# Three groups of lag between cumulative sums and their count, rests ahead of floors, and router parts on Pool

## The reference

```python
rates = relu(x) * 0.001
c = cond[:, None, :] + cumsum(rates, axis=1)
fl = floor(c)
spikes = (fl - concat([floor(cond)[:, None], fl[:, :-1]], axis=1)) / 0.001
logits = spikes.reshape(2048, 256) @ router_w.T
# softmax, the two best experts of each row, a capacity for each expert,
# gelu(rows @ w1[e]) @ w2[e], weighted by the gates and added up
out = x + ffn(spikes)
```

## Time and profile before

| | us |
|---|---|
| median of the runs | 63.9 (63.8 to 64.32) |
| the profiled execution | 64.14 |
| its span, first to last instruction | 62.4 |
| TensorE busy | 52.4 (84%) |
| VectorE busy | 34.9 (56%) |
| ScalarE busy | 27.5 (44%) |
| Pool busy | 18.9 (30%) |
| mean granted TensorE clock | 0.91 |

### The profile page before, as it was taken

The page is one execution under the profiler, slowest core; times in us unless marked ns, Lnnn a source line. Parts: engine busy times, 40 slices in busy tenths (PEclk is TensorE's granted clock), DMA queues, the critical chain, the costliest instruction groups (busy, mean ns, idle before and its releaser), DMA issues.

```text
span 62.4 us, 1154 instructions
## 1 busy us (share of the span) xinstructions
PE 52.4 (84%) x372; PEld 30.5 (49%) x372; DVE 34.9 (56%) x157; ACT 27.5 (44%) x46; POOL 18.9 (30%) x59
## 2 busy tenths in 40 slices
PE   3999999999665679999999999999999999993000
PEld 1315255546122343334296679966796666570000
DVE  3399469994677966799889529590320034036000
ACT  0499459775256779146025003940199930000000
POOL 6799875200002170064867500000000000001830
PEclk9999999999999555555699999999999999999996
DMA  0399999999999995002679834999999999200130
GB/s 0 83 365 336 345 326 366 336 360 336 349 348 347 348 348 183 16 5 66 171 250 260 289 132 92 294 362 301 364 350 354 388 384 394 95 0 0 50 98 11
DMA packets 13545, 14.82 MB, mean 238 GB/s; under 512 B 648, under 2 KB 13040, under 8 KB 13536
## 3 DMA queue, kind: packets, MB, share of 16 engines
q1 hardware_dynamic: 12608, 12.62, 62.0%
q0 software_dynamic: 816, 2.01, 10.5%
q10 hardware_dynamic: 112, 0.07, 0.5%
HBM read 13.08 MB, written 2.36 MB: 248 GB/s over the span
## 4 chain that ended last, share of the span: by engine, by line
PE 59%; DMA 11%; DVE 10%; issue 6%; ACT 4%; POOL 3%; ACTq 1%; POOLq 0%; DVEq 0%
PE bank L710 23%; PE bank L694 12%; DMA w_got<-in_L_ffn_w_dram,w_index 7%; DMA router_rows<-in_L_ffn_router_w_dram 5%; PE bank L534 4%; POOL out_dram L522 3%; PE bank L565 3%; PE bank L555 2%; PE bank L574 2%; DVE floors L963 2%; PE bank L726 2%; PE bank L545 2%; PE bank L562 2%; ACTq L797 1%; PE bank L727 1%
## 5 line engine op out<-in xcount | busy, mean ns | idle before, releaser
L534 PE MATMUL bank<-ones_b 128*128 128x512 bf16 x33 | 14.5, 568 | 1.1 <-POOL ones_b L422 1.1
L710 PE MATMUL bank<-w_sb,spare_sb 128*64 128x256 f32 x128 | 14.7, 382 | 0.0
L710 PEld LDWEIGHTS bank<-w_sb,spare_sb 128*64 128x64 f32 x128 | 8.8, 137 | 4.5
L522 POOL DMA_INDIRECT out_dram<-floors,out_index x2 | 2.0, 1016 | 22.6 <-DVE floors L1164 22.3
L853 ACT ACTIVATE spare_sb<-bank 128x512 f32<-128x512 f32 x8 | 4.6, 592 | 8.5 <-PE bank L694 8.5
L694 PE MATMUL bank<-ev_pair,w_got 128*128 128x128 f32 x64 | 7.8, 278 | 0.1
L694 PEld LDWEIGHTS bank<-ev_pair,w_got 128*128 128x128 f32 x64 | 7.4, 192 | 0.7 <-DMA w_got<-in_L_ffn_w_dram,w_index 0.7
L1071 DVE TENSOR_SCALAR rate<-bank,pair_gate 128x256 f32<-128x256 f32 x4 | 1.9, 484 | 9.5 <-PE bank L710 9.5
L503 POOL DMA_INDIRECT w_got<-in_L_ffn_w_dram,w_index x4 | 4.1, 1023 | 5.5 <-DVE w_index L1060 4.9
L534 PEld LDWEIGHTS bank<-ones_b 128*128 128x128 bf16 x33 | 3.2, 119 | 4.4 <-issue 3.2
L812 ACT ACTIVATE x_hi<-x_sb 128x512 fp32r<-128x512 f32 x7 | 4.2, 623 | 1.5 <-DMA x_sb<-in_x_dram 1.5
(11 more groups left out here) (220 smaller groups left out, 80.2 us busy)
## 6 DMA issues: line engine op xcount, KB each, us to landing
w_sb<-in_L_ffn_w_dram SPq DMA_DIRECT2D x8, 1024.0 KB, 10.9
x_sb<-in_x_dram SPq DMA_DIRECT2D x8, 256.0 KB, 5.9
out_dram<-x_sb SPq DMA_DIRECT2D x1, 2048.0 KB, 14.0
cond<-in_cond_dram ACTq DMA_DIRECT2D x2, 32.0 KB, 2.2
w_got<-in_L_ffn_w_dram,w_index POOLq DMA_INDIRECT x4, 5.2
cond<-in_cond_dram SPq DMA_DIRECT2D x1, 32.0 KB, 1.9
x_rows<-in_x_dram,out_index POOLq DMA_INDIRECT x2, 3.7
out_dram<-floors,out_index POOLq DMA_INDIRECT x2, 2.8
```

What stands on the lines that cost most here:

```text
L534: nc.tensor.matmul(bank[2][:, 0:4 * P], ones_b[:, :], ones_b[:, :].unsqueeze(1).to_broadcast([P, 4, P]), start=True, stop=True)
L710: mm = nc.tensor.matmul(Y[d % 2][at, :], hT[:, d % 2, f, at], w2_sb[:, 2 * d + side, f, :], start=(f == 0), stop=(f == FC - 1))
```

## The change

TensorE's order, ScalarE's order and VectorE's order in the sum stage are written anew, and the five router operations move from VectorE to Pool, behind the indirect DMA of line 487 and ahead of `more_lists`. `weigh(g)` now follows `cumulate(g + 3)`. The number of matmuls, rests and floors is the same. On Pool each of the five operations waits for the one before by a semaphore of its own, and the first by `router_out`, which VectorE's copy of the router sets; that copy now stands ahead of `take_rests(1)`.

```diff
+    LAG = 3
...
+            pool.wait_ge(router_out, 1)
+            g.tensor_scalar(router_s[:, :, :], routerT[:, :, :], SPIKE, 0.0, ALU.mult, ALU.add).then_inc(router_parts, 1)
+            pool.wait_ge(router_parts, 1)
+            g.tensor_copy(router3[:, 0, :, :], router_s[:, :, :]).then_inc(router_parts, 1)
+            pool.wait_ge(router_parts, 2)
+            g.tensor_tensor(router_r[:, :, :], router_s[:, :, :], router3[:, 0, :, :], ALU.subtract).then_inc(router_parts, 1)
+            pool.wait_ge(router_parts, 3)
+            g.tensor_copy(router3[:, 1, :, :], router_r[:, :, :]).then_inc(router_parts, 1)
+            pool.wait_ge(router_parts, 4)
+            g.tensor_tensor(router3[:, 2, :, :], router_r[:, :, :], router3[:, 1, :, :], ALU.subtract).then_inc(router3_set, 1)
             pool.wait_ge(counts_set, 1)
...
             for g in range(XG):
                 cumulate(g)
-                if g:
-                    weigh(g - 1)
-            weigh(XG - 1)
+                if g >= LAG:
+                    weigh(g - LAG)
+            for g in range(XG - LAG, XG):
+                weigh(g)
...
             take_rates(3)
+            take_rates(4)
             sign_floors(1)
-            take_rates(4)
             take_rates(5)
...
-            take_rests(1)
-            take_floors(0)
-            take_rests(2)
             dve.wait_ge(router_t, 1)
             v.tensor_copy(routerT[:, :, :], bank[5][:, 0:KC * E].rearrange("p (k e) -> p k e", k=KC)).then_inc(router_out, 1)
+            take_rests(1)
+            take_rests(2)
             take_rests(3)
+            take_floors(0)
+            take_rests(4)
+            take_rests(5)
             take_floors(2)
-            take_rests(4)
-            dve.wait_ge(router_out, 1)
-            loose(v.tensor_scalar(router_s[:, :, :], routerT[:, :, :], SPIKE, None, ALU.mult))
-            take_rests(5)
-            dve.wait_ge(vec, steps[0])
-            loose(v.tensor_copy(router3[:, 0, :, :], router_s[:, :, :]))
+            take_rests(6)
+            take_rests(7)
             take_floors(4)
-            dve.wait_ge(vec, steps[0])
-            loose(v.tensor_tensor(router_r[:, :, :], router_s[:, :, :], router3[:, 0, :, :], ALU.subtract))
-            take_rests(6)
-            dve.wait_ge(vec, steps[0])
-            loose(v.tensor_copy(router3[:, 1, :, :], router_r[:, :, :]))
-            take_rests(7)
-            dve.wait_ge(vec, steps[0])
-            v.tensor_tensor(router3[:, 2, :, :], router_r[:, :, :], router3[:, 1, :, :], ALU.subtract).then_inc(router3_set, 1)
             take_floors(7)
```

More of the change, by code:

```diff
@@ L252, in adaln_ffn_kernel @@
         router3_set = sem("router3_set")
+        router_parts = sem("router_parts")
         rates = sem("rates")
```

## The result

The changed kernel took 63.26 us (median of six runs, 62.85 to 63.6) against 64.06 us for the kernel before in the same comparison: ratio 0.9887, interval 0.9848 to 0.9927, that is 0.72 us less by the ratio and 0.80 by the two medians. The forecast was 63.1 us and 0.8 us less. Two later comparisons, on two chips, gave more: 0.9749 (0.9703 to 0.9796) and 0.9715 (0.9656 to 0.9774), some 1.6 and 1.8 us less.

The account below looks back on a forecast made before the run. The prediction saw one serial chain through TensorE's sum stage, about 1.8 us of it waits, with x's arrival the second limit. Stage -0.90, Pool 0 and clock +0.1 gave -0.8: from 63.9 to 63.1 us, range 62.4 to 63.9.

Parts of the forecast that it names:

- The stage: Stage of cumulative sums on TensorE: the new orders end it at 15.90 instead of 16.80, 0.90 us earlier.
- Two lo sums waited: Sign in the new trace's sum stage: only one or two lo sums on TensorE still wait for their rests.
- The arrival of x 3 fixes 10.66: Sum stage: group 3's x transfer sets when its theta matmuls end, 10.66, which no reordering moves.
- far bound: Sum stage: the most it could gain, 1.24 us, if rests 4 and 6 were never late.
- Group 0 unchanged: Start of the sum stage: group 0 still ends at 8.26, as it depends on nothing that moved.
- Pool's queue: Five router operations on Pool: 2.3 us, done near 13.7, covered by its 7.6 us idle stretch, so no cost.
- Pool against VectorE: Pool's router work beside VectorE's rests in the sum stage: could cost VectorE 0 to 0.9 us, taken as 0.
- upper bound of the prediction: Rests 5, 6 and 7 beside Pool: three holds of up to 0.40 us, less 0.3 slack, up to 0.9.
- The clock: TensorE's clock rise near `hidden(0)`: may come late once work moves 0.9 us earlier; taken as 0.1 us lost.
- rival 3: TensorE reaches `hidden(0)` earlier, the clock rise doesn't follow, all of it runs at half speed: 1.15 worse, 65.0; chance 0.10.
- The sum: Whole kernel: -0.90 for the sum stage, 0 for Pool and 0.1 for the clock make -0.8 us.

Follow-up runs that it names:

- e1: The kernel before with LAG = 3 in TensorE's order alone, the other engines in their old orders: ratio 0.9996 to the kernel before.
- e2: The changed kernel with LAG = 1, so TensorE counts a group's floors one group later, as before: ratio 1.0306 to the kernel before.
- e6: The changed kernel with ten more Pool operations, read by nobody, ahead of the far-row gather: ratio 0.9775 to the kernel before.
- e5: The changed kernel run again without alteration, on chip 2: ratio 0.9749 to the kernel before.
- e4: The kernel before with only the five router operations moved from VectorE to Pool: ratio 1.0027 to the kernel before.
- e10: The changed kernel with the five router operations put back on VectorE, on chip 3: ratio 0.9718 to the kernel before.
- e3: The changed kernel with the five router operations put back on VectorE, on chip 1: ratio 0.9859 to the kernel before.
- e9: The changed kernel a third time without alteration, on chip 3: ratio 0.9715 to the kernel before.
- e12: The changed kernel with the router operations back on VectorE, while Pool computes the same five into tiles nobody reads: ratio 0.9760 to the kernel before.

## Why the prediction was right, point by point

**The stage.** It was stepped from 8.26 with x 3 passed at 8.54, the values of the one trace I had, to an end at 15.90. The rule fitted to the later traces gives for these two values the later of 15.21 and 15.85. The gain of 0.90 was therefore right, as far as this rule tells, for the execution it was made for, and so were its parts: a group costs 0.70 and a count 0.22 in every trace, and a lo sum that waits 0.39 to 0.50. In the first trace of the changed kernel groups 2 to 7 end at 9.83, 10.53, 11.67, 12.59, 13.52 and 14.46, where I had 9.66, 10.66, 11.86, 12.79, 13.79 and 14.72. Group 3 is earlier because the pass on x 3 started 0.2 earlier, group 6 because rest 6 wasn't late. Two lo sums waited, as said.

**What I took as fixed.** "The arrival of x 3 fixes 10.66" was the step that doesn't carry over. The pass on x 3 started anywhere from 6.93 to 8.54, and the trace I had was the latest of fourteen. With the pass on x 3 at 7.2 the new order ends, by the rule and the 8.54 of the old one, 1.3 to 1.6 us ahead, for group 0 from 7.25 to 8.25. The ratios 0.9749 and 0.9715 say 1.6 and 1.8, at the upper end of this or above it, but the intervals cover it. My far bound, 1.24, was computed with x 3 at 8.54 and so was too small for those occasions. That the first comparison came out as forecast fits x being late there too: it was in both of its traces, the latest two of the fourteen, though for the runs without a trace this isn't shown. It was luck as much as reckoning.

**Group 0 unchanged.** It is unchanged by the edit but not from run to run: 7.24 to 8.25.

**Lag and order.** The prediction added the parts up along one timeline and never said that neither pays alone. e1 (0.9996) and e2 (1.0306) show it.

**Pool's queue.** Five operations were to take 2.3 us and end near 13.7; in the first trace they took 2.19 from 12.05 to 14.24, and singly 0.20 to 0.22 where no rest ran. Covered, as said.

**Pool against VectorE.** I took 0 out of 0 to 0.9. Beside rests Pool's operations grew to 0.71 and 0.53 while the rests kept their time, and VectorE lost 0.15 in two rests with far more of Pool's work beside them (e6). The rule of the Trainium skill (SBUF — State Buffer, "SBUF: two separate sides") that the two exclude each other is borne out by Pool's stretched operations. That it speaks against this change is not: of the two it was mostly Pool that was held. A likely reason, which no run isolates, is that a rest takes 0.68 and Pool's operation 0.2, so that a rest is mostly the one already running.

VectorE can be the one that is held, and the slow cast of the earlier trace rows was. In thirteen of the fourteen traces it starts 0.15 us after a Pool operation (`fine_row`) and takes 0.65, as in the first trace of the changed kernel, where that operation runs from 5.11 to 5.51:

```profile
5.26 0.65 DVE L960 CAST theta_mid<-theta_r 32x256 bf16<-32x256 f32 x1
```

In e5 it starts when Pool's operation is over (Pool, then VectorE) and takes less than half:

```profile
4.95 0.40 POOL L451 TENSOR_SCALAR fine_row<-channel_row 1x256 bf16<-1x256 bf16 x1
5.66 0.30 DVE L960 CAST theta_mid<-theta_r 32x256 bf16<-32x256 f32 x1
```

So the upper bound of the prediction was built on a real hold of 0.35 us. But the cast has one SBUF input, and the rule as the prediction tells it is about operations with two; that the cast agrees with it was too much to say.

**The clock.** I took 0.1 for a rise that comes late. Granted clock in stretches of the changed kernel (columns as in the earlier trace rows):

```profile
28.50:29.00 0.50, 0.50 (x6) 0.26 (x5) 0.45 (x4) 0.00 (x0) 0.24 (x1) 0.50 0.55 221
29.00:29.25 0.25, 0.25 (x2) 0.12 (x1) 0.21 (x3) 0.00 (x0) 0.20 (x1) 0.57 0.60 246
29.25:29.50 0.25, 0.25 (x3) 0.02 (x1) 0.21 (x3) 0.00 (x0) 0.25 (x1) 1.00 0.33 131
```

It was back a full microsecond before `hidden(0)` (30.26). Fall and rise came at 18.98 and 29.22, both 1.49 us earlier than before (20.47 and 30.71), which is more than the 0.89 by which `hidden(0)` moved. In all fourteen traces the clock was back 0.4 to 4.4 us before `hidden(0)`. The term is 0, and rival 3 didn't occur.

**The sum.** -0.90 + 0 + 0.1 = -0.8 against -0.72 measured (-0.80 by the medians). The agreement is closer than the terms deserve. Between the two traces the stage's end moved by 1.16, of which 0.77 is group 0 and not the edit; the clock's 0.1 was not paid; and 0.48 us were lost where no term of mine stood, to the gather (0.23) and the expert stage (0.25). The gather's part varies from 4.07 to 4.43 us over all traces whatever the order. Whether the expert stage's part has to do with the change is open (last section).

## What to carry to other kernels

When three engines feed one another in fixed orders, move the orders together: lag alone gave nothing, rests first alone cost 3%, both gave 1 to 3%. (The run with rests first has ScalarE's new order too; alone, that was not run.) Step the new order forward from its two or three anchors and keep the anchors apart (here the end of group 0 and the arrival of x 3), for the old order may hang on one and the new one on the other; a forecast from a single trace holds for that trace's anchors only. More traces of the old kernel could have shown it: e1 and e4, which keep VectorE's old order, have the pass on x 3 at 6.9 and group 0 at 7.25 and 8.07. Moving work off an engine pays only where that engine sets the end: by the traces 0.21 us where VectorE did (e10 against e5), and nothing where TensorE did (e3 against e9, 6.98 and 6.96).

## What the runs showed of the hardware that I had not expected

- Group 0 ends the later, the later TensorE's clock rises. With the granted clock at full from 4.0 to 4.6 us group 0 ends at 7.24 or 7.25, from 5.2 at 7.35, from 5.3 at 7.48, from 5.7 at 7.67, from 6.2 at 7.86, from 6.5 to 6.7 at 8.06 to 8.11, from 6.8 to 7.0 at 8.24 or 8.25. What TensorE does until then is the same in all of them, and in the old order all of this microsecond came through to the end of the stage. The times are those of the first entry of each trace's clock record. Tables of stretches print 1.00 ahead of it, where there is no entry, but the three warm-up matmuls ahead of group 0 show the lower level: first the kernel before (6.8), then e5 (4.0):

```profile
5.09 1.46 PE L534 MATMUL bank<-ones_b 128*128 128x512 bf16 x3
```

```profile
4.93 0.82 PE L546 MATMUL bank<-ones_b 128*128 128x512 bf16 x3
```

- The event chain from the last count to the gather took 10.03 to 10.10 us where the clock fell 4.7 us or more after the last count, and 10.17 to 10.22 where it fell earlier (e6, where `more_lists` queues behind Pool's extra work, 10.41).
- The expert stage took 24.26 to 24.28 us in six traces and 24.51 to 24.73 in eight. In the longer ones ScalarE's second gelu of the first pair starts 1.2 to 1.4 us late, and TensorE waits for it. First e5, then e12 (ScalarE in order of time):

```profile
30.24 0.60 ACT L866 ACTIVATE spare_sb<-bank 128x512 f32<-128x512 f32 x1 [3.43 <-PE bank L707]
32.50 0.60 ACT L866 ACTIVATE spare_sb<-bank 128x512 f32<-128x512 f32 x1 [1.66 <-PE bank L707]
```

```profile
30.27 0.60 ACT L869 ACTIVATE spare_sb<-bank 128x512 f32<-128x512 f32 x1 [3.45 <-PE bank L710]
31.16 0.60 ACT L869 ACTIVATE spare_sb<-bank 128x512 f32<-128x512 f32 x1 [0.30 <-PE bank L710]
```

  The same kernel (e3, e10) had it once and once not, so it doesn't follow from the program alone. But none of the four traces with VectorE's old order or with lag 1 has it, and eight of the ten with lag 3 and rests first do, all three of the changed kernel among them. So the change may bring it on, at a cost of 0.25 to 0.47 us, or the chip may: the four on the first chip (e1 to e4) are all without it. The nine traces of the changed kernel and of chips 2 and 3, e12 with them, also hold fewer semaphore events (990 to 1005 against 1059 to 1061). The cause stays open.
